# Letting the gather of node rows add them in SBUF, in place of a VectorE addition

## The chip, the cores and the metric

The kernel runs on one NeuronCore of a Trainium2 chip. The metric is the device time of one execution in microseconds (us). The median of three runs is 3204.89 us (3204.49 to 3209.08).

## What is computed

A graph attention layer over 6,250 nodes and 200,000 edges sorted by destination, with 8 heads of 16 numbers each, then a residual addition and a layer norm. Cut to what matters:

```python
q, k, v = (layer_norm(x_node @ W) per head)             # per node
ke, ve  = (layer_norm(x_edge @ W) per head)             # per edge
rel_k = layer_norm(concat([ke, k[:, src]], -1) @ relk_W + relk_b)
qk = sum(q[:, dst] * rel_k, -1) / 4
lse = segment_logsumexp(qk, dst)
rel_v = layer_norm(concat([ve, v[:, src]], -1) @ relv_W + relv_b)
h = (qk - lse[:, dst]) * rel_v
agg = segment_sum(h, dst)
z = layer_norm(relu(agg @ z_W + z_b))
out = layer_norm(x + z)
```

The product of a concatenation is a sum of two products. So what enters `rel_k` and `rel_v` of an edge is a part that comes from the edge (a projection, scaled by the edge's own reciprocal deviations) plus a part that comes from its source node. The node part is worked out once for every node and kept as a row of a table in HBM, `node_table`. This sum of the two parts is what the change is about.

## The kernel before

There are three stages. The first (lines 138 to 940, about 197 us) makes the node table, the table of q rows and the indices. The second, `edges`, is the loop over the edges and holds most of the time (from about 197 to 2936 us). The third, `tail`, forms the segment sums and the output. Since a layer norm takes the mean away, a head's 16 numbers are held by 15 coordinates (`C = 15`), so a row of the node table is 8 heads x 2 (key part, value part) x 15 = 240 floats of 32 bits.

**The loop.** A group is 512 edges, 4 tiles of 128 edges on the partitions; there are 391 groups. Every engine runs its own program `body(c, i, loop)` for c = 0, 1, 2, ...; in one body an engine works on several groups at different stages, and `x = c - 4` in the code means "the group that came in four bodies ago". 25 bodies are peeled off at the start and the rest runs in a hardware loop of 12 bodies a turn. The order of an engine's work inside a body is the order in which it is written; each step waits on semaphores and engines run in order. A group passes these steps that matter here:

- TensorE transposes the edge features (L1145), projects them for the edge variance (`y`, L1123) and again for the value that is used (`u`, L1123 through `project`, in body x + 3). It spreads the q rows over edges through a code matrix (L1136, L1172, L1179, body x + 5) and sums h by destination in the tile (L1116, body x + 10).
- ScalarE squares y (L1230), makes the reciprocal deviation `yr` (L1237, L1258), and in body x + 5 squares the finished sum p into z (L1223). Later it makes the deviations `zr` and `zw` (L1265, L1274, L1275).
- VectorE sums y's squares (L1426), and in body x + 4 scales u by yr into `p` (L1408, `s_p`). In body x + 5 it adds the gathered rows to p (L1371, `s_pt`). In body x + 6 it multiplies p by the spread q (L1389) and sums squares and products over the coordinates (L1399). In body x + 9 it forms qk (L1380) and h (L1416).
- GpSimd, in body x + 3, issues four indirect DMAs (`gathers`, L1301), each of which fetches 128 rows of the node table into the buffer `rows`, by indices in `gcol`. Two are issued at the head of a body and two at its end, and between them stand two small products of 32 numbers a partition: `zw[...,1]` (L1314, for group c - 9) and `qk0` (L1321, for group c - 8).
- SyncE issues the plain DMAs: edge features (L1051), the features of the code matrices and the gather indices (`feat` and `gcol`, after a wait on `s_ohp` and `s_pt`), four DMAs of q rows (L1077, body x + 1), and the stores of the tile sums (L1082).

`p` has 6 buffers of [4 tiles, 8 heads, 2 parts, 16]; the sixteenth number of each row is set to 1.0 once, before the loop, and stays so. `rows` has 3 buffers, z has 3.

In the profile, DMA queue q0 holds the indirect DMAs of GpSimd and q1 the plain ones of SyncE.

In `tail`, 13 indirect DMAs at L1552 scatter rows of 248 floats into the tile sums in HBM with `compute_op=ALU.add`, that is, the DMA adds the rows to what is there. L1559 and L1575 gather rows without an addition.

## Time and profile before

| | |
|---|---|
| median of 3 runs | 3204.89 us (3204.49 to 3209.08) |
| the profiled execution | 3209.04 us, its span 3207.3 us |
| instructions in the span | 75878 |
| PE (TensorE) busy | 2937.6 us, 92% |
| DVE (VectorE) busy | 2978.3 us, 93% |
| ACT (ScalarE) busy | 2307.1 us, 72% |
| POOL (GpSimd) busy | 2576.2 us, 80% |
| mean granted TensorE clock | 0.975 of full speed |
| DMA | 715.95 MB, 223 GB/s over the span |

PEld is TensorE's loading of weights, which runs beside its products. SPq, POOLq and so on are DMAs issued from an engine's queue. Busy times of an engine do not hold its waits or the issuing of plain DMAs. An indirect DMA on POOL is shown with the time in which GpSimd writes its descriptors, not with the time in which the data move. "Idle before <-releaser" names what the engine waited for; "issue" is time in which it waited for nothing that the profile shows.

### The profile page before, as it was taken

The page shows a single profiled execution, that of the slowest core. Times are in us where ns is not written, and L with a number is a line of the kernel's source. Part 1 is how long each engine was busy: PE and PEld are TensorE (multiplying, and loading weights), DVE is VectorE, ACT ScalarE, POOL GpSimd, SP SyncE. Part 2 cuts the span into 40 slices and gives each one's busy share as a digit, 9 for nine tenths or more (in the row PEclk, how much of TensorE's full clock was granted, in tenths as well). Part 3 has the DMA queues.
Part 4 walks back from the last instruction along what each step waited for, and adds up shares of the span by engine and source line. Part 5 has one row for each costly group of instructions (what it writes and reads, how often), then busy time and mean ns, then how long its engine had stood idle before and what let it go on. Part 6 is the DMA issues. An engine that isn't in the chain of part 4 may idle for free. (4 is left out here: it accounts for less than half of the span.)

```text
span 3207.3 us, 75878 instructions
## 1 busy us (share of the span) xinstructions
PE 2937.6 (92%) x18674; PEld 2485.6 (77%) x18870; DVE 2978.3 (93%) x3387; ACT 2307.1 (72%) x5276; POOL 2576.2 (80%) x2622
## 2 busy tenths in 40 slices
PE   5669999999999999999999999999999999996955
PEld 3358888888888888888888888888888888885633
DVE  7879999999999999999999999999999999996957
ACT  2457777777777777777777777777777777775536
POOL 7768888888888888888888888888888888883773
PEclk9989999999999999999999999999999999999976
DMA  3568887778787778777778777778777777785642
GB/s 86 160 180 237 240 243 240 242 238 243 239 243 239 243 238 243 239 243 240 241 239 244 238 244 238 243 238 244 239 242 240 241 240 241 242 246 176 178 123 76
DMA packets 660921, 715.95 MB, mean 223 GB/s; under 512 B 97993, under 2 KB 554430, under 8 KB 660469
## 3 DMA queue, kind: packets, MB, share of 16 engines
q1 hardware_dynamic: 568201, 499.33, 51.8%
q0 software_dynamic: 84896, 211.42, 21.8%
q10 hardware_dynamic: 7756, 4.43, 0.6%
q8 instruction: 26, 0.43, 0.1%
q14 instruction: 42, 0.34, 0.0%
HBM read 482.62 MB, written 231.46 MB: 223 GB/s over the span
## 5 line engine op out<-in xcount | busy, mean ns | idle before, releaser
L1301 POOL DMA_INDIRECT e_rows<-node_table,e_gcol x1564 | 2093.0, 1338 | 422.2 <-issue 419.9
L1123 PE MATMUL banks<-w_edge,e_eat 128*128 128x240 f32 x6256 | 1435.9, 373 | 57.9 <-DVE e_p L1408 50.6
L1123 PEld LDWEIGHTS banks<-w_edge,e_eat 128*128 128x128 f32 x6256 | 1156.7, 190 | 281.2 <-DVE e_p L1408 207.1
L1116 PE MATMUL banks<-e_h,e_oh 128*128 128x248 f32 x3128 | 805.5, 380 | 9.4 <-ACT e_agg L1200 5.3
L1399 DVE TENSOR_REDUCE e_zs<-e_z 128x96 f32<-128x1440 f32 x391 | 646.1, 1653 | 40.2 <-DVE e_z L1389 7.8
L1209 ACT ACTIVATE e_oht<-banks 128x512 bf16<-128x512 f32 x391 | 233.5, 597 | 476.8 <-remote 240.2
L1116 PEld LDWEIGHTS banks<-e_h,e_oh 128*128 128x128 f32 x3128 | 533.6, 190 | 43.5 <-DVE e_h L1416 6.2
L1200 ACT ACTIVATE e_agg<-banks 128x496 f32<-128x496 f32 x782 | 455.3, 582 | 95.7 <-PE banks L1116 95.7
L1408 DVE TENSOR_TENSOR e_p<-banks,e_yr 128x960 f32<-128x960 f32 x391 | 448.8, 1148 | 3.3 <-PE banks L1123 3.3
L1416 DVE TENSOR_TENSOR e_h<-e_p,e_zw 128x960 f32<-128x960 f32 x391 | 448.9, 1148 | 1.2 <-POOL e_zw L1314 1.2
L1371 DVE TENSOR_TENSOR e_p<-e_p,e_rows 128x960 f32<-128x960 f32 x391 | 449.1, 1149 | 0.0
L1426 DVE TENSOR_REDUCE e_yvar<-e_ysq 128x64 f32<-128x960 f32 x391 | 447.6, 1145 | 0.0
L1230 ACT ACTIVATE e_ysq<-banks 128x960 f32<-128x960 f32 x391 | 379.7, 971 | 54.7 <-PE banks L1123 5.6
L1223 ACT ACTIVATE e_z<-e_p 128x960 f32<-128x960 f32 x391 | 389.8, 997 | 0.0
L1179 PE MATMUL banks<-e_q,e_oht 128*128 128x128 bf16 x4692 | 325.8, 219 | 2.8 <-DVE e_z L1389 2.8
L1389 DVE TENSOR_TENSOR e_z<-e_p,banks 128x512 f32<-128x512 f32 x391 | 269.0, 688 | 51.7
L1179 PEld LDWEIGHTS banks<-e_q,e_oht 128*128 128x128 bf16 x4692 | 278.3, 98 | 3.3 <-issue 3.2
L1145 PEld LDWEIGHTS banks<-ident,e_ea 128*128 128x128 f32 x1564 | 195.6, 141 | 94.8 <-DMA e_ea<-in_edge_attr 25.3
L1145 PE MATMUL banks<-ident,e_ea 128*128 128x128 f32 x1564 | 235.8, 273 | 33.7 <-DMA e_ea<-in_edge_attr 23.5
L1215 ACT ACTIVATE e_eat<-banks 128x512 f32<-128x512 f32 x391 | 231.5, 592 | 18.2 <-PE banks L1145 18.2
L1244 ACT ACTIVATE e_oh<-banks 128x512 f32<-128x512 f32 x391 | 229.7, 587 | 0.0
L1172 PE MATMUL banks<-rank_code,e_feat 128*128 128x128 bf16 x1564 | 151.1, 219 | 0.0
(413 smaller groups left out, 2596.6 us busy)
## 6 DMA issues: line engine op xcount, KB each, us to landing
tile_sums<-e_agg SPq DMA_DIRECT2D x391, 496.0 KB
e_q<-q_by_rank SPq DMA_DIRECT2D x1564, 96.0 KB
e_ea<-in_edge_attr SPq DMA_DIRECT2D x390, 256.0 KB
e_rows<-node_table,e_gcol POOLq DMA_INDIRECT x1564
edge_lse<-t_lse_sb SPq DMA_DIRECT2D x14, 448.0 KB, 3.6
edge_qk<-e_qkt SPq DMA_DIRECT2D x130, 48.0 KB
node_table<-n_tb SPq DMA_DIRECT2D x24, 240.0 KB, 2.8
n_x<-in_x SPq DMA_DIRECT2D x24, 128.0 KB, 2.3
```

The source lines that it names most:

```text
L1116: last = nc.tensor.matmul(agg_ps[:, (j % 2) * AW:(j % 2 + 1) * AW], oh[:, x % OR, j, :], hh[:, x % HR, j, :, :].rearrange("p h e -> p (h e ...
L1123: last = nc.tensor.matmul(out_ps[:, j // 2, (j % 2) * 2 * HC:(j % 2 + 1) * 2 * HC], eat[:, x % 4, j * P:(j + 1) * P], t["w_edge"][:, at:at ...
L1145: last = nc.tensor.transpose(eat_ps[:, j * P:(j + 1) * P], ea[:, k, j, :], ident[:])
L1179: last = nc.tensor.matmul(qx_ps[:, j * F:(j + 1) * F], oht[:, x % 2, j * P:(j + 1) * P], qw[:, k, j, part * F:(part + 1) * F], start=(part ...
L1200: nc.scalar.activation(agg[:, k, 2 * half:2 * half + 2, :].rearrange("p j c -> p (j c)"), agg_ps[:, 0:2 * AW], ACT.Copy).then_inc(s_ags, 1)
L1223: nc.scalar.activation(z[:, x % ZR, :, 0:2 * H, 0:C], p[:, k, :, :, :, 0:C].rearrange("p t h k c -> p t (h k) c"), ACT.Square).then_inc(s_ ...
L1301: g.indirect_dma_start(out=rows[:, k, j, :], out_offset=None, in_=table, in_offset=bass.IndirectOffsetOnAxis(ap=gcol[:, kb, at:at + 1].bit ...
L1371: v.tensor_tensor(out=p[:, k, :, :, :, 0:C].rearrange("p t h k c -> p (t h k) c"), in0=p[:, k, :, :, :, 0:C].rearrange("p t h k c -> p (t ...
L1399: v.tensor_reduce(out=zs[:, x % WR, :, :], in_=z[:, x % ZR, :, :, 0:C], axis=AX.X, op=ALU.add).then_inc(s_z, 1)
L1408: v.tensor_tensor(out=p[:, k, :, :, :, 0:C].rearrange("p (b t) h k c -> p b (t h k) c", b=2), in0=u_ps.rearrange("p b (h c) -> p b h c", c=C),
L1416: v.tensor_tensor(out=hh[:, x % HR, :, :, 0:2 * C].rearrange("p t h (s c) -> p (t h) s c", s=2), in0=p[:, k, :, :, 1, 0:C].rearrange("p t ...
L1426: v.tensor_reduce(out=yvar[:, x % 2, :, :], in_=ysq[:, x % 2, :, :].rearrange("p t (h c) -> p t h c", c=C), axis=AX.X, op=ALU.add).then_in ...
```

## The change

The rows of the node table are now added to p by the DMA that fetches them. For this a table row is laid out as p is, with 16 numbers a head of which the last is zero: 256 floats, 1,024 bytes in place of 960. The first stage clears the sixteenth numbers of its buffer once and writes the 15 others with a stride; its store moves 1,024 bytes a row.

In the loop, `gathers` moves from body x + 3 to body x + 4, writes to `p` with `compute_op=ALU.add`, and waits for `s_p` (VectorE's scaled product of the same group, L1408). The buffer `rows`, the addition at L1371 and its semaphore `s_pt` go; readers of p wait for the gather's semaphore `s_ga`, which now has one for each of p's 6 buffers. ScalarE's square (L1223), VectorE's product with q (L1389) and the reduction (L1399), TensorE's code matrices (L1136, L1172, L1179), SyncE's q rows (L1077) and ScalarE's steps on `zs` (L1265 to L1275) all come one body later. The product `qk0` comes one body later too, and both small products are VectorE's now, at the head of its body and after the reduction. GpSimd has nothing left but the gathers, four in a row. SyncE's wait before it reloads `gcol` is on `s_psq`, ScalarE's square.

```diff
--- before.py
+++ after.py
@@ -56,7 +56,7 @@
-        table = dram("node_table", [N, 2 * HC])
+        table = dram("node_table", [N, 2 * F])
...
@@ -260,7 +260,7 @@
-    tb = sb("n_tb", [P, 3, 2, 2 * HC])
+    tb = sb("n_tb", [P, 3, 2, 2 * H, D])
...
@@ -388,7 +388,8 @@
                     b, nb, rows = pair(n)
                     sp.wait_ge(s_tb, n + 1)
-                    sp.dma_start(table[P * b:P * b + nb * rows, :].rearrange("(b p) f -> p b f", p=rows), tb[0:rows, n % 3, 0:nb, :]).then_inc(s_tst[n % 3], 16)
+                    sp.dma_start(table[P * b:P * b + nb * rows, :].rearrange("(b p) f -> p b f", p=rows),
+                                 tb[0:rows, n % 3, 0:nb, :, :].rearrange("p b h d -> p b (h d)")).then_inc(s_tst[n % 3], 16)
             for k in range(3):
...
@@ -684,6 +685,7 @@
 
             dve.wait_ge(s_pool2, ALL_MASKS)
+            link(v.memset(tb[:, :, :, :, C:D], 0.0))
...
@@ -707,8 +709,8 @@
                     dve.wait_ge(s_u, n + 1)
-                    v.tensor_tensor(out=tb[0:rows, n % 3, 0:nb, :], in0=tb[0:rows, n % 3, 0:nb, :],
-                                    in1=t["table_bias"][0:rows].unsqueeze(1).to_broadcast([rows, nb, 2 * HC]), op=ALU.add).then_inc(s_tb, 1)
+                    v.tensor_tensor(out=tb[0:rows, n % 3, 0:nb, :, 0:C], in0=tb[0:rows, n % 3, 0:nb, :, 0:C],
+                                    in1=t["table_bias"][0:rows].rearrange("p (h c) -> p h c", c=C).unsqueeze(1).to_broadcast([rows, nb, 2 * H, C]), op=ALU.add).then_inc(s_tb, 1)
                 n = c - 2
                 if pair(n):
                     b, nb, rows = pair(n)
@@ -716,7 +718,7 @@
                         dve.wait_ge(s_tst[n % 3], 16 * (n // 3))
-                    v.tensor_tensor(out=tb[0:rows, n % 3, 0:nb, :].rearrange("p b (h c) -> p b h c", c=C),
+                    v.tensor_tensor(out=tb[0:rows, n % 3, 0:nb, :, 0:C],
                                     in0=second[n % 2][0:rows, 0:nb * 2 * HC].rearrange("p (b h c) -> p b h c", b=nb, c=C),
                                     in1=rstd[0:rows, n % 2, 0:nb, H:3 * H].unsqueeze(3).to_broadcast([rows, nb, 2 * H, C]), op=ALU.mult).then_inc(s_u, 1)
...
@@ -946,7 +948,7 @@
     sb, sem = ph.sb, ph.sem
-    EA, QR, RR, PR, HR, OR, AG, ZR, WR = 4, 6, 3, 6, 6, 6, 4, 3, 4
+    EA, QR, PR, HR, OR, AG, ZR, WR = 4, 6, 6, 6, 6, 4, 3, 4
...
@@ -956,7 +958,6 @@
     yln = sb("e_yln", [P, TILES, 2 * H])
     yr = sb("e_yr", [P, 2, TILES, 2 * H])
-    rows = sb("e_rows", [P, RR, TILES, 2 * HC])
...
@@ -986,12 +987,12 @@
-    s_ga = [sem(f"gathered{i}") for i in range(RR)]
+    s_ga = [sem(f"rows_added{i}") for i in range(PR)]
...
     s_y, s_ysq, s_yv, s_yl, s_yr = sem("y_projected"), sem("y_squared"), sem("y_summed"), sem("y_ln"), sem("y_rstd")
-    s_u, s_p, s_pt, s_psq = sem("u_projected"), sem("p_scaled"), sem("rows_added"), sem("p_squared")
+    s_u, s_p, s_psq = sem("u_projected"), sem("p_scaled"), sem("p_squared")
     s_ohtp, s_oht, s_ohp, s_oh = sem("oht_coded"), sem("oht_ready"), sem("oh_coded"), sem("oh_ready")
...
@@ -1063,10 +1064,10 @@
                             sp.wait_ge(s_ohp, used)
-                            sp.wait_ge(s_pt, used)
+                            sp.wait_ge(s_psq, used)
                         sp.dma_start(feat[0:3, kb, :], t["feat_d"][:, bass.ds(BE * b, BE)]).then_inc(s_ft[kb], 16)
                         sp.dma_start(gcol[:, kb, :], t["cols"][:, bass.ds(BATCH * TILES * b, BATCH * TILES)]).then_inc(s_ft[kb], 16)
-                x = c - 1
+                x = c - 2
                 if is_group(x, loop):
                     n, k = UNROLL * i + x, x % QR
...
@@ -1125,7 +1126,7 @@
 
             def body(c, i, loop):
-                x = c - 4
+                x = c - 5
...
@@ -1163,7 +1164,7 @@
                     nc.tensor.transpose(eat_ps[0:H * TILES * ng, 0:P], src, ident[:]).then_inc(s_qkt, 1)
-                x = c - 5
+                x = c - 6
                 if is_group(x, loop):
...
@@ -1200,7 +1201,7 @@
             def body(c, i, loop):
-                x = c - 4
+                x = c - 5
                 if is_group(x, loop):
...
@@ -1214,10 +1215,10 @@
                 copy_sums(c - 10, i, loop, 0)
-                x = c - 5
+                x = c - 6
                 if is_group(x, loop):
                     n, k = UNROLL * i + x, x % PR
-                    act.wait_ge(s_pt, n + 1)
+                    act.wait_ge(s_ga[k], 64 * use(x, i, PR))
                     if loop or x >= ZR:
                         act.wait_ge(s_z, n - ZR + 1)
@@ -1235,7 +1236,7 @@
                     nc.scalar.activation(yln[:], yvar[:, x % 2, :, :], ACT.Ln, bias=t["eps_c"][:, 0:1], scale=1.0 / D).then_inc(s_yl, 1)
-                x = c - 5
+                x = c - 6
                 if is_group(x, loop):
...
@@ -1256,7 +1257,7 @@
                     nc.scalar.activation(yr[:, x % 2, :, :], yln[:], ACT.Exp, scale=-0.5).then_inc(s_yr, 1)
-                x = c - 7
+                x = c - 8
                 if is_group(x, loop):
...
@@ -1264,7 +1265,7 @@
                 copy_sums(c - 10, i, loop, 1)
-                x = c - 7
+                x = c - 8
                 if is_group(x, loop):
...
@@ -1290,37 +1291,21 @@
             def gathers(x, i, loop, first):
 
                 if is_group(x, loop):
-                    n, k, kb = UNROLL * i + x, x % RR, (x // BATCH) % FB
+                    n, k, kb = UNROLL * i + x, x % PR, (x // BATCH) % FB
                     if first == 0:
                         pool.wait_ge(s_ft[kb], 32 * (i + (x // BATCH) // FB + 1))
-                        if loop or x >= RR:
-                            pool.wait_ge(s_pt, n - RR + 1)
+                        pool.wait_ge(s_p, n + 1)
                     pool.reg_add(last_node, nodes_less_2, 1)
                     for j in (first, first + 1):
                         at = (x % BATCH) * TILES + j
-                        g.indirect_dma_start(out=rows[:, k, j, :], out_offset=None, in_=table,
+                        g.indirect_dma_start(out=p[:, k, j, :, :, :].rearrange("p h k d -> p (h k d)"), out_offset=None, in_=table,
                                              in_offset=bass.IndirectOffsetOnAxis(ap=gcol[:, kb, at:at + 1].bitcast(u32), axis=0),
-                                             bounds_check=last_node, oob_is_err=True).then_inc(s_ga[k], 16)
+                                             bounds_check=last_node, oob_is_err=True, compute_op=ALU.add).then_inc(s_ga[k], 16)
 
             def body(c, i, loop):
-                gathers(c - 3, i, loop, 0)
-                x = c - 9
-                if is_group(x, loop):
-                    n = UNROLL * i + x
-                    pool.wait_ge(s_qk, n + 1)
-                    pool.wait_ge(s_zw, n + 1)
-                    if loop or x >= WR:
-                        pool.wait_ge(s_h, n - WR + 1)
-                    g.tensor_tensor(out=zw[:, x % WR, :, :, 1], in0=hh[:, x % HR, :, :, 2 * C], in1=zw[:, x % WR, :, :, 0], op=ALU.mult).then_inc(s_w2, 1)
-                x = c - 8
-                if is_group(x, loop):
-                    n = UNROLL * i + x
-                    pool.wait_ge(s_zr, n + 1)
-                    if loop or x >= 1:
-                        pool.wait_ge(s_qk, n)
-                    g.tensor_tensor(out=qk0[:], in0=zs[:, x % WR, :, 2 * H:3 * H], in1=zr[:, x % WR, :, 0:H], op=ALU.mult).then_inc(s_qk0, 1)
-                gathers(c - 3, i, loop, 2)
-            every(pool, body, GROUPS + 9)
+                gathers(c - 4, i, loop, 0)
+                gathers(c - 4, i, loop, 2)
+            every(pool, body, GROUPS + 4)
 
         @block.vector
         def _(dve):
@@ -1363,13 +1348,23 @@
             link(v.tensor_tensor(out=cen[:, 1, :, :], in0=cen[:, 0, :, :], in1=t["rows16"][:, ZG, :].unsqueeze(1).to_broadcast([P, H, D]), op=ALU.mult))
 
             def body(c, i, loop):
-                x = c - 5
+                x = c - 9
+                if is_group(x, loop):
+                    n = UNROLL * i + x
+                    dve.wait_ge(s_zr, n + 1)
+                    if loop or x >= 1:
+                        dve.wait_ge(s_qk, n)
+                    v.tensor_tensor(out=qk0[:], in0=zs[:, x % WR, :, 2 * H:3 * H], in1=zr[:, x % WR, :, 0:H], op=ALU.mult).then_inc(s_qk0, 1)
+                x = c - 7
                 if is_group(x, loop):
                     n, k = UNROLL * i + x, x % PR
-                    dve.wait_ge(s_ga[x % RR], 64 * use(x, i, RR))
-                    dve.wait_ge(s_p, n + 1)
-                    v.tensor_tensor(out=p[:, k, :, :, :, 0:C].rearrange("p t h k c -> p (t h k) c"), in0=p[:, k, :, :, :, 0:C].rearrange("p t h k c -> p (t h k) c"),
-                                    in1=rows[:, x % RR, :, :].rearrange("p t (h c) -> p (t h) c", c=C), op=ALU.add).then_inc(s_pt, 1)
+                    dve.wait_ge(s_ga[k], 64 * use(x, i, PR))
+                    dve.wait_ge(s_qx, n + 1)
+                    if loop or x >= ZR:
+                        dve.wait_ge(s_z, n - ZR + 1)
+                        dve.wait_ge(s_qk, n - ZR + 1)
+                    v.tensor_tensor(out=z[:, x % ZR, :, 2 * H:3 * H, :], in0=p[:, k, :, :, 0, :],
+                                    in1=qx_ps.rearrange("p (t h d) -> p t h d", t=TILES, d=D), op=ALU.mult).then_inc(s_pq, 1)
                 x = c - 9
                 if is_group(x, loop):
                     n = UNROLL * i + x
@@ -1378,17 +1373,7 @@
                         dve.wait_ge(s_agg, 2 * (n - HR) + 2)
                         dve.wait_ge(s_qkt, batch(x - HR, i) + 1)
                     v.tensor_tensor(out=hh[:, x % HR, :, :, 2 * C], in0=qk0[:], in1=z[:, x % ZR, :, 2 * H:3 * H, C], op=ALU.add).then_inc(s_qk, 1)
-                x = c - 6
-                if is_group(x, loop):
-                    n, k = UNROLL * i + x, x % PR
-                    dve.wait_ge(s_pt, n + 1)
-                    dve.wait_ge(s_qx, n + 1)
-                    if loop or x >= ZR:
-                        dve.wait_ge(s_z, n - ZR + 1)
-                        dve.wait_ge(s_qk, n - ZR + 1)
-                    v.tensor_tensor(out=z[:, x % ZR, :, 2 * H:3 * H, :], in0=p[:, k, :, :, 0, :],
-                                    in1=qx_ps.rearrange("p (t h d) -> p t h d", t=TILES, d=D), op=ALU.mult).then_inc(s_pq, 1)
-                x = c - 6
+                x = c - 7
                 if is_group(x, loop):
                     n = UNROLL * i + x
                     dve.wait_ge(s_psq, n + 1)
@@ -1397,6 +1382,14 @@
                         dve.wait_ge(s_zl, n - WR + 1)
                         dve.wait_ge(s_qk0, n - WR + 1)
                     v.tensor_reduce(out=zs[:, x % WR, :, :], in_=z[:, x % ZR, :, :, 0:C], axis=AX.X, op=ALU.add).then_inc(s_z, 1)
+                x = c - 9
+                if is_group(x, loop):
+                    n = UNROLL * i + x
+                    dve.wait_ge(s_qk, n + 1)
+                    dve.wait_ge(s_zw, n + 1)
+                    if loop or x >= WR:
+                        dve.wait_ge(s_h, n - WR + 1)
+                    v.tensor_tensor(out=zw[:, x % WR, :, :, 1], in0=hh[:, x % HR, :, :, 2 * C], in1=zw[:, x % WR, :, :, 0], op=ALU.mult).then_inc(s_w2, 1)
                 x = c - 4
                 if is_group(x, loop):
                     n, k = UNROLL * i + x, x % PR
```

## Rows read from the trace of the kernel before

**Rows 1.** Busy time of each engine from 1500 to 2000 us, in the loop.
```profile
1500.00:2000.00 500.00, 487.84 (x3211) 421.99 (x3246) 482.93 (x504) 387.69 (x887) 421.55 (x431) 1.00 0.79 241
```
**Rows 2.** Timeline of VectorE, a little over one group.
```profile
start us, us, engine line op out<-in xcount [idle before <-releaser]
1502.93 1.15 DVE L1371 TENSOR_TENSOR e_p<-e_p,e_rows 128x960 f32<-128x960 f32 x1
1504.00 0.21 DVE L1380 TENSOR_TENSOR e_h<-e_qk,e_z 128x32 f32<-128x32 f32 x1
1504.34 0.69 DVE L1389 TENSOR_TENSOR e_z<-e_p,banks 128x512 f32<-128x512 f32 x1
1505.12 1.65 DVE L1399 TENSOR_REDUCE e_zs<-e_z 128x96 f32<-128x1440 f32 x1
1506.69 1.15 DVE L1408 TENSOR_TENSOR e_p<-banks,e_yr 128x960 f32<-128x960 f32 x1
1507.76 1.15 DVE L1416 TENSOR_TENSOR e_h<-e_p,e_zw 128x960 f32<-128x960 f32 x1
1508.82 1.15 DVE L1426 TENSOR_REDUCE e_yvar<-e_ysq 128x64 f32<-128x960 f32 x1
1509.88 1.15 DVE L1371 TENSOR_TENSOR e_p<-e_p,e_rows 128x960 f32<-128x960 f32 x1
```
**Rows 3.** Timeline of GpSimd, over the same stretch.
```profile
1503.15 1.81 POOL L1301 DMA_INDIRECT e_rows<-node_table,e_gcol  x1 [0.30 <-issue]
1504.99 0.30 POOL L1314 TENSOR_TENSOR e_zw<-e_h,e_zw 128x32 f32<-128x32 f32 x1
1505.23 0.26 POOL L1321 TENSOR_TENSOR e_qk<-e_zs,e_zr 128x32 f32<-128x32 f32 x1
1505.65 1.04 POOL L1301 DMA_INDIRECT e_rows<-node_table,e_gcol  x1 [0.16 <-issue]
1506.99 1.03 POOL L1301 DMA_INDIRECT e_rows<-node_table,e_gcol  x1 [0.30 <-issue]
1508.32 1.47 POOL L1301 DMA_INDIRECT e_rows<-node_table,e_gcol  x1 [0.30 <-issue]
```
**Rows 4.** Waits from 1500 to 2000 us: total us, times, longest us.
```profile
PEld banks L1123 <- DVE e_p L1408: 38.2, 72, 0.7
```
**Rows 5.** Timeline of the tail, GpSimd and VectorE, around the scatters that add.
```profile
2970.44 1.15 DVE L1650 TENSOR_TENSOR t_ratio<-t_m 128x896 f32<-128x896 f32 x1
2970.47 1.63 POOL L1552 DMA_INDIRECT tile_sums<-firsts,carry_idx  x1 [21.06 <-ACT firsts L1871]
...
2977.79 1.09 DVE L1651 TENSOR_TENSOR t_ratio<-t_ratio,t_fresh 128x896 f32<-128x896 f32 x1
2978.29 2.02 POOL L1552 DMA_INDIRECT tile_sums<-firsts,carry_idx  x1 [0.30 <-issue]
...
2990.74 1.56 POOL L1552 DMA_INDIRECT tile_sums<-firsts,carry_idx  x1 [0.30 <-issue]
2990.87 1.09 DVE L1650 TENSOR_TENSOR t_ratio<-t_m 128x896 f32<-128x896 f32 x1 [1.79 <-PE banks L2006]
...
2994.82 1.63 POOL L1552 DMA_INDIRECT tile_sums<-firsts,carry_idx  x1 [0.30 <-issue]
```
**Rows 6.** Source line L1552: duration ns min/median/max, and landing time.
```profile
L1552 POOL DMA_INDIRECT tile_sums<-firsts,carry_idx x13: 1556/1663/2020, 2970.5 to 2994.8; - x13
DMA to landing us min/median/max: 10.2/12.3/14.2
```
**Rows 7.** DMA queues, loop, 1500 to 2000 us: packets, MB, share of 16 engines.
```profile
q1 hardware_dynamic: 95496, 85.09, 56.7%
q0 software_dynamic: 13778, 35.28, 22.6%
```
**Rows 8.** DMA queues, tail, 2970 to 3008 us.
```profile
q0 software_dynamic: 1872, 1.65, 30.1%
```
**Rows 9.** Timeline: the loop's first scaled product, its last gather, its last VectorE operation.
```profile
212.44 1.16 DVE L1408 TENSOR_TENSOR e_p<-banks,e_yr 128x960 f32<-128x960 f32 x1 [2.14 <-PE banks L1123]
...
2913.56 1.02 POOL L1301 DMA_INDIRECT e_rows<-node_table,e_gcol  x1 [0.30 <-issue]
...
2934.60 1.16 DVE L1416 TENSOR_TENSOR e_h<-e_p,e_zw 128x960 f32<-128x960 f32 x1 [0.40 <-POOL e_zw L1314]
```

## The prediction, made before the change was run

> **What bounds the kernel now.** I read first the busy times of a stretch in the loop's middle. In 500 us TensorE is busy for 487.84 us, VectorE for 482.93 us, and the 16 DMA engines 79% of the time, all at the full granted clock [rows 1]. So nothing has much room, and the period of a group has to be read from the timelines. From one L1371 on VectorE to the next it is 1509.88 - 1502.93 = 6.95 us [rows 2]. 391 groups of it are 2717 us of the span of 3207.3 us.
>
> VectorE's seven operations follow each other with no idle time to speak of; from start to start the five of 960 or more elements take 1.06 to 1.57 us. Its only gaps are latencies of its own, such as the 0.34 us from L1380 to L1389, of which L1380 is 0.21 us [rows 2]. TensorE is nearly full, but not the bound: before the projection at L1123 the weight loads wait 38.2 / 72 = 0.53 us a group for L1408 on VectorE [rows 4].
>
> GpSimd deserves the longest look. It never waits for another engine: its four gathers, two products and the 0.30 us of issue before a gather fill the period [rows 3]. But the gathers differ. Two take 1.03 and 1.04 us, one 1.47 us, one 1.81 us. The one of 1.81 us starts at 1503.15, inside L1371, which gives way to the next operation at 1504.00: 0.85 us later. The one of 1.47 us starts at 1508.32, inside L1416, which gives way 0.50 us later. So a gather costs 1.03 us, and when it starts inside a VectorE operation with both inputs in SBUF it is held until that ends [rows 2, 3]. GpSimd is locked to VectorE's rhythm, with VectorE as the pace maker.
>
> **The change, part by part.**
>
> *VectorE.* L1371 goes: 1504.00 - 1502.93 = 1.07 us a group. Two products of 32 numbers come. The like of them is L1380, with 0.21 us, up to 0.34 us where the next waits for its end [rows 2]. As operations overlap by some 0.08 us (L1408 lasts 1.15 us, L1416 starts after 1.07), each costs 0.13 to 0.34 us. The rest is L1389 0.78, L1399 1.57, L1408 1.07, L1416 1.06 and L1426 1.06, together 5.54 us; with three small ones 5.9 to 6.6 us. VectorE alone would allow a period of about 6.1 us.
>
> *TensorE.* Nothing is added. Without the wait of 0.53 us its period would be 6.95 - 0.53 = 6.42 us [rows 4]. It would be next after VectorE.
>
> *GpSimd, the term that decides.* It loses two products (0.30 and 0.26 us, overlapping) and gets four gathers that add. The loop has no such DMA, but the tail has 13: L1552 scatters 128 rows of 248 floats with the same addition. The free one among them, started at 2990.74 before the next VectorE operation, took 1.56 us. One started 0.5 us before the end of L1651 took 2.02 us, and the median is 1.66 us [rows 5, 6]. From the first start to the last are 24.35 us for 12, that is 2.03 us each, issue and holds included [rows 5]. Against 1.03 us for a plain gather the descriptors of an adding DMA cost half as much again. A scatter adds in HBM and this gather adds in SBUF; bounds for its price are 1.03 us (nothing extra) and 2.02 us. I take 1.56 us, because both kinds read one side, read the other and write it.
>
> Four times (1.56 + 0.30) = 7.44 us, with nothing between them. To that comes what L1416 holds up: it is now the only long VectorE operation with both inputs in SBUF (L1371 is gone; L1389, L1408 read PSUM). It lasts 1.06 us, starts of gathers lie 1.86 us apart, so a start falls inside it in 57% of phases and then waits 0.53 us on average: 0.31 us, with 0 and 1.06 us as bounds. The period is 7.75 us, bounds 7.44 and 8.50.
>
> A rule speaks on this hold. The trace shows +0.44 us on a gather that starts inside L1416 [rows 2, 3]. The Trainium skill, "SBUF — State Buffer", section "Who interferes with whom", infers that generating descriptors needs only the write side of the shared port, so that a tensor_tensor does not stall a DMA. By that there would be no hold here and 3412 us in all. For the plain gathers the trace contradicts it.
>
> *DMA engines.* In the loop the plain queue takes 56.7% and the gathers' queue 22.6% of 16 engines [rows 7]; per group of 6.95 us that is 3.94 and 1.57 us. The 13 adding scatters took 30.1% of 38 us [rows 8], 11.4 us for 13 or 0.88 us each, so four take 3.52 us, and with rows of 1024 in place of 992 bytes 3.63 us. Together 7.57 us a group. The lower bound is no extra but the bytes (1.57 x 1024/960 = 1.67, together 5.61 us). I take 7.57 us, which is under 7.75 us, but by little: the engines would be 98% busy.
>
> *The new wait.* A gather waits for `s_p`; only gathers are queued behind it. Its data then come late: L1552 landed 12.3 us after its start at the median [rows 6]. From L1408 of a group the circle is gathers (7.2 us), landing (at most 12.3), ScalarE's square and its steps to the next yr, L1408 of the group three later (1.15). ScalarE is busy for 387.69/500 of 6.95 us, 5.4 us [rows 1]; I put those steps at 3.5 us of it, an estimate. That is 24.15 us for three periods, so 8.05 us is its bound with that landing, and 6 us with one of half the length. It costs nothing unless landings are as slow as in the tail.
>
> *The rest.* The later stages of all engines move by one body together; SyncE's q rows keep their distance to their reader, and its wait on `s_psq` has four buffers of slack. Costs nothing. In the first stage a memset of 96 numbers costs under 0.7 us (L1389 takes 0.69 us for 512) [rows 2], the table's stores grow by 7% and lie beside other work. At the loop's start GpSimd no longer runs ahead: its first gather follows the first L1408, which ends at 213.6 us. At the end, the last gather ended at 2914.6 us and VectorE at 2935.8 us [rows 9]; now some 16 us pass from the last descriptors to that point. What lies behind, 3207.3 - 2935.8 = 271.5 us, and the 1.7 us between span (3207.3) and time (3209.0) stay. So the time is 213.6 + 16 + 271.5 + 1.7 + 391 x period, about 503 + 391 x period. For 6.95 us the formula gives 3220, near the 3209 us of the profiled run, which is 4 us over the median. With 7.75 us it gives **3533 us**, 10% slower.
>
> **Rivals.**
>
> *Faster: descriptors and engines both cheap (6%).* If an adding gather in SBUF takes GpSimd 1.03 us, four make 5.3 us, 6.4 with a full hold by L1416. If its data also need little more than now, the DMA engines allow 5.6 us. Then TensorE sets the period at 6.42 us: 503 + 2510 = 3013 us. The point from which it decides: under 1.36 us per gather, where 4 x (1.36 + 0.30) + 0.31 = 6.95 us is today's period, and under 3.0 us of DMA time for four. Against it stand all 13 rows of the kind, none under 1.556 us [rows 6]. No change at all (1%) would need this to be met by chance.
>
> *The DMA engines are the bound while descriptors are cheap (8%):* 7.57 us, 3463 us. For it: the 98% above.
>
> *Both at once (15%):* engines so full that landings last 12 us and more; then the circle of the new wait or the queue holds the loop. With 12.3 us the circle gives 8.05 us or 3651 us; with 14.2 us [rows 6] 8.68 us or 3897 us. For it: landings in the tail, 10.2 us at the least. Against it: big plain transfers ran beside them there.
>
> *The lock is always hit (8%):* GpSimd and VectorE fall into step so that a gather starts with L1416 each time, as happens now twice a group: 8.50 us, 3827 us.
>
> *No hold at all (10%):* 7.44 us, 3412 us. For it: an adding scatter that started 0.03 us after L1650 still took only 1.63 us. Against it: the one of 2.02 us [rows 5]. This is what the sentence of the Trainium skill's "SBUF — State Buffer" quoted above would make of it.
>
> *The forecast (52%):* between 7.5 and 8.1 us.
>
> **How the numbers follow.** The forecast is the likeliest case. The range goes from the case of 7.2 us, a little under the DMA bound (503 + 2815 = 3318), to the fully held lock and the slower half of the full engines, 3840 us. Left out are the faster case (6%), a sliver of the cheap ones and the slowest landings, 15 to 20% in all. A difference under 0.2% can't be told from none here. Faster 6%, same 1%, slower 93%.
>
> **What would show it.** Right: L1301's successor at 1.55 to 1.7 us where unheld; GpSimd's idle before it only issue, 0.30 us, with the four filling 7.5 to 8 us; VectorE idle about 1.5 us a group before L1389, waiting for the gather's landing; TensorE busy near 88%; DMA share above 0.9. Wrong: gathers near 1.03 us, or GpSimd waiting on L1408 (then the circle or the DMA engines bind), or one packet a row not appearing in the gathers' queue, whose 98 ns a packet (0.301 x 38 x 16 / 1872 us) [rows 8] is behind my 3.5 us.

## The result and the profile after

The changed kernel takes 3510.61 us (median of 4 runs, 3502.56 to 3515.71) against 3205.47 us, a ratio of 1.0947, 95% interval [1.0924, 1.0971]. It is slower by 305 us, 9.5%. The forecast was 3533 us. The profiled execution has a span of 3506.4 us.

The busy times of the loop's middle, in the order span, TensorE, weight loads, VectorE, ScalarE, GpSimd, granted clock, DMA share, GB/s. It answers to [rows 1]:

```profile
1500.00:2000.00 500.00, 451.94 (x2944) 391.59 (x2943) 382.92 (x519) 344.43 (x796) 421.03 (x260) 0.98 0.99 222
```

TensorE and VectorE have lost ground, the DMA share has gone from 0.79 to 0.99, and GpSimd ran 260 gathers, that is 65 groups: 500 / 65 = 7.69 us a group in place of 6.95. Now some 7 us of GpSimd, as in [rows 3], with them VectorE, as in [rows 2], and one square of ScalarE:

```profile
1506.20 1.55 POOL L1301 DMA_INDIRECT e_p<-node_table,e_gcol  x1 [0.30 <-issue]
1507.85 0.19 DVE L1357 TENSOR_TENSOR e_qk<-e_zs,e_zr 128x32 f32<-128x32 f32 x1 [2.49 <-ACT e_zr L1275]
1508.03 0.69 DVE L1366 TENSOR_TENSOR e_z<-e_p,banks 128x512 f32<-128x512 f32 x1
1508.06 1.55 POOL L1301 DMA_INDIRECT e_p<-node_table,e_gcol  x1 [0.30 <-issue]
1508.64 0.21 DVE L1375 TENSOR_TENSOR e_h<-e_qk,e_z 128x32 f32<-128x32 f32 x1
1508.81 1.65 DVE L1384 TENSOR_REDUCE e_zs<-e_z 128x96 f32<-128x1440 f32 x1
1509.92 1.55 POOL L1301 DMA_INDIRECT e_p<-node_table,e_gcol  x1 [0.31 <-issue]
1510.38 0.20 DVE L1392 TENSOR_TENSOR e_zw<-e_h,e_zw 128x32 f32<-128x32 f32 x1
1510.50 1.15 DVE L1401 TENSOR_TENSOR e_p<-banks,e_yr 128x960 f32<-128x960 f32 x1
1511.56 1.15 DVE L1409 TENSOR_TENSOR e_h<-e_p,e_zw 128x960 f32<-128x960 f32 x1
1511.78 2.35 POOL L1301 DMA_INDIRECT e_p<-node_table,e_gcol  x1 [0.30 <-DVE e_p L1401]
1511.95 1.01 ACT L1224 ACTIVATE e_z<-e_p 128x960 f32<-128x960 f32 x1 [2.38 <-DMA e_p<-node_table,e_gcol]
1512.63 1.14 DVE L1419 TENSOR_REDUCE e_yvar<-e_ysq 128x64 f32<-128x960 f32 x1
```

The lines have moved: L1366 is the old L1389, L1384 the old L1399, L1401 the old L1408, and ScalarE's L1224 the old L1223. A gather takes 1.55 us where it took 1.03. The one that starts at 1511.78, 0.22 us after VectorE began L1409 (the old L1416), takes 2.35 us: VectorE goes on to L1419 at 1512.63, 0.85 us after the gather's start, and the gather is 0.80 us longer. VectorE itself now has time, here 2.49 us before a group's first operation.

The waits of the stretch (total us, times, longest), and the DMA queues (packets, MB, share of 16 engines), which answer to [rows 4, 7]:

```profile
ACT e_z L1224 <- DMA e_p<-node_table,e_gcol: 130.2, 58, 4.6
DVE e_qk L1357 <- ACT e_zr L1275: 115.2, 54, 4.5
POOL e_p L1301 <- issue: 75.3, 247, 0.3
POOL e_p L1301 <- DVE e_p L1401: 4.0, 13, 0.3
```

```profile
q1 hardware_dynamic: 86568, 77.00, 51.1%
q0 software_dynamic: 37278, 33.95, 47.6%
```

ScalarE waits 2.0 us a group for the gathered data and VectorE waits 1.8 us for ScalarE. The 4.0 us of GpSimd that stand against VectorE are 13 idle times of 0.3 us, no longer than the gap before any other gather, so GpSimd waits for nobody: 421.03 us of work and 79.3 us of such gaps fill the stretch. The gathers' queue takes 0.476 x 7.69 = 3.66 us a group, in place of 1.57, in 37278 packets where the kernel before had 13778 in the same time.

The first gather and the last VectorE operation of the loop, as in [rows 9]:

```profile
213.10 1.65 POOL L1301 DMA_INDIRECT e_p<-node_table,e_gcol  x1 [16.75 <-DVE e_p L1401]
3214.56 1.55 POOL L1301 DMA_INDIRECT e_p<-node_table,e_gcol  x1 [0.30 <-issue]
3233.84 1.16 DVE L1409 TENSOR_TENSOR e_h<-e_p,e_zw 128x960 f32<-128x960 f32 x1
```

From 213.10 to 3216.11 us are 3003.0 us for 391 groups, 7.68 us each, and 18.9 us of drain follow.

The theory to be tested (A): the time that GpSimd needs to write the descriptors of an adding gather sets the period. Its rivals: the 16 DMA engines are full (B); the circle of gathers, landing, square and scaled product sets it (C); the new order itself costs (R).

### The profile page after: what moved, and what is told of

It reads as the page before. It is cut to its first block and busy times, and to the rows that moved or that the text cites. A ratio compares the mean times of both kernels' runs of the same rounds, so it can differ in the third digit from the quotient of the medians.

```text
span 3506.4 us, 75086 instructions
## 1 busy us (share of the span) xinstructions
PE 3008.3 (86%) x18870; PEld 2542.7 (73%) x18870; DVE 2656.2 (76%) x3779; ACT 2273.8 (65%) x5276; POOL 2804.2 (80%) x1840
## 5 line engine op out<-in xcount | busy, mean ns | idle before, releaser
L1301 POOL DMA_INDIRECT e_p<-node_table,e_gcol x1564 | 2526.4, 1615 | 493.4 <-issue 457.7
L1124 PEld LDWEIGHTS banks<-w_edge,e_eat 128*128 128x128 f32 x6256 | 1208.8, 194 | 105.4 <-DVE e_p L1401 7.5
L1224 ACT ACTIVATE e_z<-e_p 128x960 f32<-128x960 f32 x391 | 392.8, 1005 | 791.5 <-DMA e_p<-node_table,e_gcol 790.6
L1117 PE MATMUL banks<-e_h,e_oh 128*128 128x248 f32 x3128 | 856.0, 397 | 15.8 <-ACT e_agg L1201 13.3
L1384 DVE TENSOR_REDUCE e_zs<-e_z 128x96 f32<-128x1440 f32 x391 | 646.1, 1652 | 4.4 <-ACT e_z L1224 0.3
L1117 PEld LDWEIGHTS banks<-e_h,e_oh 128*128 128x128 f32 x3128 | 546.2, 195 | 96.0 <-ACT e_agg L1201 32.6
L1357 DVE TENSOR_TENSOR e_qk<-e_zs,e_zr 128x32 f32<-128x32 f32 x391 | 74.8, 191 | 696.1 <-ACT e_zr L1275 686.8
L1401 DVE TENSOR_TENSOR e_p<-banks,e_yr 128x960 f32<-128x960 f32 x391 | 448.7, 1148 | 5.8 <-PE banks L1124 5.7
L1409 DVE TENSOR_TENSOR e_h<-e_p,e_zw 128x960 f32<-128x960 f32 x391 | 449.1, 1149 | 0.2
L1419 DVE TENSOR_REDUCE e_yvar<-e_ysq 128x64 f32<-128x960 f32 x391 | 447.8, 1145 | 0.1
L1137 PE MATMUL banks<-e_feat,rank_code 128*128 128x512 bf16 x391 | 149.5, 382 | 290.4 <-ACT e_oh L1245 289.8
L1137 PEld LDWEIGHTS banks<-e_feat,rank_code 128*128 128x128 bf16 x391 | 37.7, 96 | 381.0 <-issue 324.8
L1366 DVE TENSOR_TENSOR e_z<-e_p,banks 128x512 f32<-128x512 f32 x391 | 268.6, 687 | 12.4 <-DMA e_p<-node_table,e_gcol 3.2
L1146 PE MATMUL banks<-ident,e_ea 128*128 128x128 f32 x1564 | 248.9, 283 | 22.0 <-DMA e_ea<-in_edge_attr 22.0
L1146 PEld LDWEIGHTS banks<-ident,e_ea 128*128 128x128 f32 x1564 | 179.9, 143 | 86.0 <-DMA e_ea<-in_edge_attr 22.8
```

The source lines that it names most:

```text
L1117: last = nc.tensor.matmul(agg_ps[:, (j % 2) * AW:(j % 2 + 1) * AW], oh[:, x % OR, j, :], hh[:, x % HR, j, :, :].rearrange("p h e -> p (h e ...
L1124: last = nc.tensor.matmul(out_ps[:, j // 2, (j % 2) * 2 * HC:(j % 2 + 1) * 2 * HC], eat[:, x % 4, j * P:(j + 1) * P], t["w_edge"][:, at:at ...
L1146: last = nc.tensor.transpose(eat_ps[:, j * P:(j + 1) * P], ea[:, k, j, :], ident[:])
L1224: nc.scalar.activation(z[:, x % ZR, :, 0:2 * H, 0:C], p[:, k, :, :, :, 0:C].rearrange("p t h k c -> p t (h k) c"), ACT.Square).then_inc(s_ ...
L1301: g.indirect_dma_start(out=p[:, k, j, :, :, :].rearrange("p h k d -> p (h k d)"), out_offset=None, in_=table, in_offset=bass.IndirectOffse ...
L1384: v.tensor_reduce(out=zs[:, x % WR, :, :], in_=z[:, x % ZR, :, :, 0:C], axis=AX.X, op=ALU.add).then_inc(s_z, 1)
```

## Experiments

All ratios are to the kernel before, with 95% intervals. The pieces of code show the lines that matter; semaphore counts, buffers and waits that go with them are left out.

### The same kernel without the addition

```diff
-   bounds_check=last_node, oob_is_err=True, compute_op=ALU.add).then_inc(s_ga[k], 16)
+   bounds_check=last_node, oob_is_err=True).then_inc(s_ga[k], 16)
```

> The changed kernel with its gathers fetching rows into p without adding them (the sum of the two parts is left out: p holds the node rows alone). Everything else of the change stays, the rows of 1024 bytes and the products on VectorE too. Theory A (the price of an adding gather on GpSimd sets the period of 7.68 us): a gather falls from 1.55 to about 1.03 us, GpSimd and the DMA engines have room, TensorE sets 6.42 to 6.6 us a group, 503 + 391 x period = 3013 to 3085 us. Rival R (it is the new order that costs: the gather after the scaled product, one body later, and two more products on VectorE): over 3300 us.

Measured: 3056.32 us, ratio 0.9527 [0.951, 0.9544]. The one argument is worth 454 us. First GpSimd, then the busy times in the loop (the columns as above):

```profile
1503.70 1.18 POOL L1301 DMA_INDIRECT e_p<-node_table,e_gcol  x1 [1.46 <-DVE e_p L1401]
1505.18 1.01 POOL L1301 DMA_INDIRECT e_p<-node_table,e_gcol  x1 [0.31 <-issue]
1506.51 1.01 POOL L1301 DMA_INDIRECT e_p<-node_table,e_gcol  x1 [0.32 <-issue]
```

```profile
1500.00:2000.00 500.00, 498.01 (x3420) 454.83 (x3457) 452.42 (x613) 412.37 (x941) 321.42 (x306) 1.00 0.87 261
```

With rows of the same 1024 bytes and the same wait on `s_p`, a gather takes 1.01 us and GpSimd sits waiting for L1401. TensorE is busy for 498 of 500 us: it is the bound, at (3056 - 503) / 391 = 6.53 us a group. R falls: without the addition the new order is faster than the kernel before. A and B are not told apart by this run, since it takes load off GpSimd and off the DMA engines (0.87 in place of 0.99) at once; the runs with fewer and with more bytes below do that.

### The two products alone

The kernel before, with L1314 and L1321 moved to VectorE; the plain gathers and L1371 stay.

```diff
 (GpSimd)
-   g.tensor_tensor(out=zw[..., 1], ...)      # group c - 9
-   g.tensor_tensor(out=qk0[:], ...)          # group c - 8
 (VectorE, at the head of the body and after the reduction)
+   v.tensor_tensor(out=qk0[:], ...)          # group c - 9
+   v.tensor_tensor(out=zw[..., 1], ...)      # group c - 9
```

> The kernel before with one part of the change alone: the two products of 32 numbers move from GpSimd to VectorE, the addition L1371 and the plain gathers stay. Theory A: VectorE stays the bound and its period of 6.95 us grows by 0.05 to 0.35 us, 3225 to 3340 us. Rival (GpSimd had been the pace maker of the kernel before, since it never waited): faster, 3100 to 3180 us.

Measured: 3293.88 us, ratio 1.0269 [1.025, 1.0288], that is +89 us or 0.23 us a group for two products. VectorE was the pace maker of the kernel before, though GpSimd never waited: giving GpSimd less to do did not help, and in this run GpSimd does wait, 78.0 us of the 500, for L1363 (the old L1371).

### Fewer and more bytes for the DMA engines

```diff
 (fewer)
-   for j in range(TILES):
+   for j in range(1):
        sp.dma_start(qw[:, k, j, :], t["q_rank"][bass.ds(first[j], P), :]).then_inc(s_q[k], 16)
 (more, behind the four loads)
+   for j in range(2):
+       sp.dma_start(spare_q[:, k, j, :], t["q_rank"][bass.ds(first[j], P), :]).then_inc(s_q[k], 16)
```

> The changed kernel with three of the four loads of q rows a group left out (their tiles of q are zero), 288 KB a group less for the DMA engines and nothing else changed for GpSimd. Theory A (descriptors on GpSimd bind): period 7.44 to 7.70 us, 3412 to 3515 us, DMA share falls to about 0.88, gathers stay at 1.55 us. Theory B (the 16 DMA engines bind, at their share of 0.99): they lose about a quarter of the plain queue's 3.92 us, the period follows to about 6.7 to 6.9 us, 3120 to 3200 us.

> The changed kernel with two more loads of q rows a group, into a buffer that nobody reads: 192 KB a group more on the DMA engines, nothing more for GpSimd. By the queue's 3.92 us for some 1180 KB a group they cost about 0.6 us. Theory A alone, with engines whose busy share overstates them: no change, 3500 to 3530 us. If the engines are in truth as full as their share of 0.99 says, they become the bound: 7.58 + 0.6 = 8.2 us a group, about 3700 us, and GpSimd begins to wait for L1401.

Measured: with fewer bytes 3510.24 us, 1.0942 [1.0921, 1.0963], no change at all. With more bytes 3531.91 us, 1.1012 [1.0994, 1.1031], 21 us more than the change and 2 us over the expected 3500 to 3530. The queues of the two, first with fewer, then with more:

```profile
q0 software_dynamic: 37411, 34.08, 48.6%
q1 hardware_dynamic: 58636, 57.56, 37.5%
```

```profile
q1 hardware_dynamic: 104874, 89.39, 57.6%
q0 software_dynamic: 37151, 33.83, 46.3%
```

The plain queue went from 37.5 to 57.6% of the engines. The share of the whole went from 0.86 to 1.04, and the time moved by 0.6%. B falls. In the second run the plain queue took 0.576 x 7.75 = 4.46 us of the engines a group (500 us held 64.5 groups), 0.53 us more than the 0.511 x 7.69 = 3.93 us of the change, and the group became 21 / 391 = 0.05 us longer. So a busy share of 0.99 did not mean that the engines were full, and a share of 1.04 shows that it counts times of packets that overlap. Even the 21 us are seen on GpSimd: the sum of what its gathers last beyond 1.554 us (those over 1.6 us, whole loop) is 0.32 us a group in place of the change's 0.24, and from first to last gather the period is 7.76 us in place of 7.68. Why more gathers are held there (235 in place of 195) is not shown.

### More work for GpSimd

```diff
     gathers(c - 4, i, loop, 0)
+    g.tensor_tensor(out=extra[:], in0=ident[:], in1=ident[:], op=ALU.mult)
     gathers(c - 4, i, loop, 2)
```

> The changed kernel with one more operation on GpSimd a group, between its second and third gather: a product of two 128x128 tiles that nobody reads. Theory A (GpSimd is filled by its gathers and sets the period): all of it comes on top, 0.3 to 0.5 us less the 0.14 us that the issue of the next gather overlaps with it, so +0.15 to +0.4 us a group and 3570 to 3670 us. Rival C (the circle gathers, landing, square, yr, scaled product over three periods sets it): it has slack on GpSimd itself, below +0.1 us a group, 3510 to 3545 us.

Measured: 3699.79 us, 1.1522 [1.1489, 1.1556], 189 us or 0.48 us a group more than the change. The product took longer than thought, and part of it lies over the end of the gather before it:

```profile
1498.66 1.68 POOL L1303 DMA_INDIRECT e_p<-node_table,e_gcol  x1 [0.31 <-issue]
1499.84 0.93 POOL L1313 TENSOR_TENSOR e_extra<-ident 128x128 f32<-128x128 f32 x1
1500.93 1.56 POOL L1303 DMA_INDIRECT e_p<-node_table,e_gcol  x1 [0.16 <-issue]
```

The gather ends at 1500.34 and the next begins at 1500.93, 0.29 us later than after the usual 0.30 us of issue; over the stretch the mean product is 1.16 us, held by VectorE now and then. Its size was misjudged, its sign was not: what is added on GpSimd lengthens the loop, where C had slack for it. C falls. The timelines of the change say the same: past the first ten groups a group's first gather starts 2.8 to 6.5 us after its L1401 has ended, 4.65 us at the median. In the run without the addition, where GpSimd does wait for L1401, it is 0.77 us at the median.

### One, two and three of four tiles added by the DMA

```diff
+   rows = sb("e_rows", [P, RR, PLAIN, H, 2, D])
 (GpSimd)
-   gathers(c - 4, i, loop, 0)
-   gathers(c - 4, i, loop, 2)
+   plain_gathers(c - 3, i, loop)     # tiles 0 to PLAIN - 1 into rows, no addition
+   gathers(c - 4, i, loop)           # the other tiles, added into p
 (VectorE, group c - 5, behind qk0)
+   v.tensor_tensor(out=p[:, k, 0:PLAIN, :, :, 0:C], in0=p[:, k, 0:PLAIN, :, :, 0:C],
+                   in1=rows[:, x % RR, :, :, :, 0:C], op=ALU.add).then_inc(s_pt, 1)
```

> As the mixed version, but only tile 3 is added by the DMA and VectorE adds three tiles (about 0.82 us). GpSimd: 1.55 + 3 x 1.03 + 4 x 0.30 = 5.84 us plus holds of up to 1.6 us; VectorE 5.54 + 0.82 + small ones, about 6.8 us, is the bound. Theory A: 6.8 to 6.9 us, 3162 to 3200 us, between the mixed version and the kernel before. Rival (holds): as the kernel before, 3200 us.

> A mixed version: tiles 0 and 1 of a group are gathered without an addition into a buffer of their own (in body x + 3) and added by VectorE as before (half of L1371, some 0.57 us), tiles 2 and 3 are added by the DMA. GpSimd: 2 x 1.55 + 2 x 1.03 + 4 x 0.30 = 6.36 us plus holds; VectorE: 5.54 + 0.57 + three small ones, about 6.55 us; TensorE 6.54 us as in the run without any addition. Theory A: period 6.6 to 6.8 us, 503 + 391 x period = 3084 to 3162 us, faster than both kernels. Rival (holds by two VectorE operations with two SBUF inputs meet gathers in step, as in the kernel before): up to 7.1 us, 3280 us.

> As the mixed version, but with three of the four tiles added by the DMA and one by VectorE. Theory A (GpSimd's time for descriptors adds up gather by gather): 3 x 1.55 + 1.04 + 4 x 0.30 = 6.89 us plus 0.2 to 0.4 us of holds, 7.1 to 7.3 us a group, 3279 to 3357 us, between the mixed version (3057 us) and the change (3511 us). Rival (the price of adding is only felt once all four are adding, through the wait on the scaled product): near 3060 us.

| tiles added by the DMA | us | ratio | (us - 503) / 391 |
|---|---|---|---|
| 1 | 3068.98 | 0.9561 [0.9535, 0.9586] | 6.56 |
| 2 | 3056.95 | 0.9533 [0.9509, 0.9557] | 6.53 |
| 3 | 3304.07 | 1.0297 [1.0274, 1.032] | 7.16 |
| 4, the change | 3510.61 | 1.0947 [1.0924, 1.0971] | 7.69 |

From three to four the period grows by 0.53 us, close to the 1.55 - 1.03 = 0.52 us for one gather, so the price is not only felt once all four add. With two, the bound has passed to another engine; the time lies 27 us under the expected 3084 to 3162 us, because the period came down to TensorE's 6.53 us, where 6.6 us had been taken as the least. Busy times with two tiles and with one:

```profile
1500.00:2000.00 500.00, 500.00 (x3456) 454.73 (x3455) 489.49 (x688) 412.63 (x944) 407.02 (x306) 1.00 1.01 260
```

```profile
1500.00:2000.00 500.00, 500.00 (x3443) 447.41 (x3442) 498.72 (x683) 410.12 (x938) 407.33 (x305) 1.00 0.92 260
```

TensorE is busy all the time in both, and with one tile VectorE as well. GpSimd's gathers with two tiles, and below them the adding one of the run with one tile (busy us, mean ns, idle before):

```profile
L1318 POOL DMA_INDIRECT e_p<-node_table,e_gcol x153 | 238.6, 1560 | 46.6 <-issue 46.6
L1305 POOL DMA_INDIRECT e_rows<-node_table,e_gcol x153 | 169.7, 1109 | 46.6 <-issue 46.6
```

```profile
L1318 POOL DMA_INDIRECT e_p<-node_table,e_gcol x77 | 171.6, 2229 | 23.5 <-issue 23.5
```

With two tiles 238.6 + 169.7 + 93.2 us of issue fill 500 us, so three engines are level. This version beats the kernel before by 4.7% and the change by 13%. It is as fast as the run that leaves the addition out altogether, 3056.95 against 3056.32 us. Its DMA share is 1.01, at a period 1.16 us shorter than the change's.

With one tile the expectation was 3162 to 3200 us, and 3069 was measured. The step that failed is VectorE's sum: the 0.34 us from L1380 to the next operation [rows 2] is 0.17 us after L1375 above, and from L1366 to the next it is 0.61 in place of 0.78 us. By the code, an operation that waited for the one right before it now has another in between; that this is the reason is argued, not tested. GpSimd has no room with one tile either: its adding gather starts inside VectorE's addition L1380 every time and takes 2.23 us in place of 1.55. That is the prediction's rival of the lock that is always hit, and here it costs next to nothing, since the other two engines need nearly the same period.

### Without the long VectorE operation that holds gathers

```diff
-   v.tensor_tensor(out=hh[:, x % HR, :, :, 0:2 * C] ..., in0=p[...], in1=zw[...], op=ALU.mult)
+   v.tensor_tensor(out=hh[:, x % HR, :, :, 0], in0=p[:, k, :, :, 1, 0], in1=zw[:, x % WR, :, :, 1], op=ALU.mult)
```

> The changed kernel with VectorE's L1409, its only long operation with both inputs in SBUF, cut down to 32 numbers a partition; the other numbers of h are zero, so nearly all of h is left out. VectorE is not the bound, so its own 1.06 us are worth nothing. Theory H (a gather that starts inside such an operation is held until it ends, 42 of 260 gathers and 0.29 us a group): GpSimd's period falls from 7.68 to 7.4 to 7.5 us, 3396 to 3436 us, and no gather is longer than about 1.65 us. Rival (the long gathers come from something else, such as full descriptor rings): no change, 3500 to 3520 us, long gathers stay.

Measured: 3414.47 us, 1.0649 [1.0631, 1.0667], 96 us or 0.25 us a group less than the change, from an engine that was not the bound. The gathers of this run, and those of the change, in the same 500 us. In the first row, of this run, the mean is 1554 ns. In the second, of the change, the three numbers are minimum, median and maximum in ns:

```profile
L1302 POOL DMA_INDIRECT e_p<-node_table,e_gcol x269 | 418.1, 1554 | 82.0 <-issue 74.4 <-DVE e_p L1403 7.6
```

```profile
L1301 POOL DMA_INDIRECT e_p<-node_table,e_gcol x260: 1553/1554/2547, 1498.8 to 1998.8; - x130
```

The gathers over 1.6 us are gone. Set against VectorE's timeline gather by gather, the change has 42 of its 260 starts inside L1409, on average 0.50 us before VectorE's next operation, and those are 0.45 us longer; the other 218 are 1.59 us at the most. In the kernel before, 144 of 287 start inside L1371 or L1416, 0.68 us before the next operation and 0.62 us longer; the others are 1.05 us at the most. Over the whole loop of the change, 195 of 1564 gathers last over 1.6 us, and what they last beyond 1.554 us is 0.24 us a group, as much as this run saves.

## Why the prediction was right, and which steps were not

**The price of an adding gather** was the step that decided. Taken as 1.56 us from a scatter in the tail that adds in HBM [rows 5, 6], it measured 1.554 us for a gather that adds in SBUF. The runs show that this price is the cause: without the addition the loss is gone, with one adding gather less 0.53 us a group of it are gone, and neither fewer nor more bytes on the DMA engines do the like. The reason given for the equal price, that both kinds read one side, read the other and write it, was not tested; the agreement alone doesn't show it.

**The hold** was put at 0.31 us a group from lengths and spacings. The stretch above has 42 x 0.45 / 65 = 0.29 us, the whole loop 0.24 us, and the run without L1409 gives 0.25 us. It is the mis-sized term: 4 x (1.554 + 0.305) + 0.24 = 7.68 us is the measured period, for 7.75 us. Over 391 groups that is 27 us; less the longer drain (18.9 us for 16) and the 2.4 us by which the median lies over the profiled run, that is the 22 us between forecast and result. The sentence of the Trainium skill, "SBUF — State Buffer", section "Who interferes with whom", by which a tensor_tensor would not hold up the writing of descriptors, is contradicted by plain and by adding gathers alike. Plain ones that start inside such an operation are 0.62 us longer, adding ones 0.45 us.

**The DMA engines** were the step whose reading failed. The sum of 7.57 us a group was right as a busy time, 0.99 x 7.69 = 7.6 us, and so were its 98 ns a packet: 0.476 x 500 x 16 / 37278 us are 102 ns. But I read it as a bound, with 8% for "the engines are the bound" at 3463 us and 15% for engines "so full" that landings hold the loop. With two more loads a group the same sum is 1.04 x 7.75 = 8.06 us, more than the period of 7.75 us in which it was done; the run without holds went at (3414 - 503) / 391 = 7.45 us, a little below the supposed bound, with the same adding gathers; three quarters of the q loads less gave nothing.

**The new wait** cost nothing, as said: past the first ten groups, a group's first gather comes 2.8 us or more after L1401. But the landing of 12.3 us in its circle was wrong, and it was added to 7.2 us of gathers, though it is counted from the start of a DMA and the last gather's own 1.56 us lie in both. The trace of the change shows the landing. Gathers and squares are all there, so the k-th L1224 belongs to the k-th four gathers, and where it waited for the data (347 of 391 groups) it starts as they land: 3.7 to 7.2 us after the fourth gather's start, 5.4 us at the median. Above, these are 1506.20 and 1511.95. With 5.4 us the circle is (7.2 + 5.4 + 3.5 + 1.15) / 3 = 5.75 us, with the estimate of 3.5 us left as it was. The tail's landings were no guide for the loop's.

**Where VectorE is idle** came out otherwise than the prediction's sign had it. Not L1366 (the old L1389) waits for the landing, but the operation before it, L1357, for ScalarE, 115.2 / 65 = 1.8 us a group; ScalarE is the one that waits for the data.

**VectorE and TensorE.** From L1357 to L1357, waits left out, VectorE's operations take 5.84 us a group (0.18 + 0.61 + 0.17 + 1.57 + 0.12 + 1.06 + 1.07 + 1.06), just under my 5.9 to 6.6 us. TensorE's floor is 6.53 us, for 6.42 us; I had taken off the whole wait of its weight loads, part of which lay beside products: in the kernel before, weight loads waited 38.2 us for L1408 in the stretch [rows 4], products at L1123 only 8.9 us. Neither mattered for the change, both do for the mixed version.

**The formula** 503 + 391 x period held: 16 us of drain were 18.9 us, the first gather came at 213.1 us for 213.6.

## What to carry to other kernels

When work moves into a DMA that GpSimd issues, price the descriptors first. Here the addition cost 0.54 us of GpSimd's time for each 128 rows and saved VectorE 0.27 us, a quarter of L1371. An engine that never waits but is held by another (GpSimd before) has some room, though not the room that its base cost suggests; a split of the work, two tiles each way, brought three engines level and was the best of the versions that compute the whole sum. A price for an operation that the loop lacks may stand elsewhere in the same trace.

## What the runs showed of the hardware that I had not expected

The mean busy share of the 16 DMA engines is no measure of fullness here: at 0.99 (the change), at 1.01 (two tiles, 1.16 us a group faster) and at 1.04 (two more loads, 0.6% slower, by longer holds on GpSimd) it did not set the period. The adding gathers' time on the engines was 3.66 us a group, against 0.294 x 6.54 = 1.92 us without the addition, in 37278 against 14628 packets in 500 us; it was paid beside other work. The same bytes a row came in about three times as many packets a group; what of this costs GpSimd its 0.54 us is open. And that price does not hang on the load of the DMA engines: the least is 1553 ns and the median 1553 or 1554 ns at shares of 0.86, 0.99 and 1.04, and in the change's stretch no gather that starts outside L1409 is over 1.59 us.
